# Attention and a routed expert layer on one core: where VectorE's routing operations stand, and who sends the results

## What is computed

```
Q = (x @ Wq.T).reshape(B, S, HKV, G, HEAD_DIM)          # K, V alike
scores = jnp.einsum('bskgd,bswkd->bskgw', Q, K_win) * scale
attn = jax.nn.softmax(scores, axis=-1)
out = jnp.einsum('bskgw,bswkd->bskgd', attn, V_win)
x = _layernorm(x + out.reshape(B, S, HQ * HEAD_DIM) @ Wo.T)
probs_BTE = jax.nn.softmax(x @ kernel_router_DE, axis=-1)
weights_BTX, indices_BTX = jax.lax.top_k(probs_BTE, TOP_K)
norm_weights_BTX = jax.nn.softmax(weights_BTX, axis=-1)
fuse_BTEF = jax.nn.silu(gating_BTEF) * jnp.einsum('BTD,EDF->BTEF', x, kernel_up_EDF)
down_BTED = jnp.einsum('BTEF,EFD->BTED', fuse_BTEF, kernel_down_EFD)
x = _layernorm(x + jnp.einsum('BTED,BTE->BTD', down_BTED, full_weights_BTE))
```

## Time and profile before

| | us |
|---|---|
| median of 3 runs (lowest, highest) | 593.84 (588.29, 595.39) |
| the profiled execution, its own time | 593.14 |
| its span in the trace | 591.3 |
| TensorE busy | 492.1 (83%) |
| VectorE busy | 359.9 (61%) |
| ScalarE busy | 297.9 (50%) |
| GpSimd busy | 241.4 (41%) |
| mean granted TensorE clock | 0.896 of full |

### The profile page before, as it was taken

One profiled execution on the slowest core, in us unless ns is written; L12 is line 12 of the kernel. 1 busy time (PEld: TensorE's weight loads), 2 busy tenths in 40 slices (PEclk: granted clock), 3 DMA queues, 4 the chain that ended last, 5 costly groups with the idle time before them and its releaser, 6 DMA issues.

```text
span 591.3 us, 12074 instructions
## 1 busy us (share of the span) xinstructions
PE 492.1 (83%) x3864; PEld 301.5 (51%) x3864; DVE 359.9 (61%) x817; ACT 297.9 (50%) x515; POOL 241.4 (41%) x329
## 2 busy tenths in 40 slices
PE   4499899899998999899898987966988999998600
PEld 3263454354453555344453533435877888886500
DVE  0366675576675887667756566553364635767674
ACT  2125554465566656456644544534565555554532
POOL 2131062462533225325435264305714517777072
PEclk9999898798999998899977877788889999999855
DMA  6452324305216352231350012020433535553252
GB/s 159 62 81 56 73 41 105 73 11 135 38 34 147 73 108 56 56 65 54 55 84 18 20 41 86 11 63 25 127 97 96 149 110 135 137 136 96 62 137 58
DMA packets 83948, 46.93 MB, mean 79 GB/s; under 512 B 40496, under 2 KB 79408, under 8 KB 83120
## 3 DMA queue, kind: packets, MB, share of 16 engines
q1 hardware_dynamic: 77184, 36.81, 27.2%
q0 software_dynamic: 4096, 8.40, 5.2%
q10 hardware_dynamic: 2608, 0.95, 0.8%
HBM read 26.47 MB, written 19.40 MB: 78 GB/s over the span
## 4 chain that ended last, share of the span: by engine, by line
PE 61%; DVE 15%; issue 8%; DMA 6%; ACT 3%; SPq 3%; POOL 2%; ACTq 0%; POOLq 0%; DVEq 0%
PE pV L788 13%; DVE mp L1311 6%; PE pX L977 6%; PE pX L713 5%; PE pX L957 4%; PE pX L752 4%; PE pX L959 4%; PE pX L958 3%; DMA xt<-xT 3%; PE pV L968 3%; DVE rden L1359 3%; PE pM L807 3%; PE pX L743 2%; PE pX L764 2%; SPq L427 2%
## 5 line engine op out<-in xcount | busy, mean ns | idle before, releaser
L1311 DVE TENSOR_REDUCE mp<-pX 128x4 f32<-128x1024 f32 (+4 forms) x128 | 150.2, 1186 | 96.6 <-PE pX L717 80.1
L1051 ACT ACTIVATE probs<-pX 128x1024 f32<-128x1024 f32 x152 | 152.8, 1023 | 108.7 <-PE pX L743 94.4
L788 PE MATMUL pV<-probs,vx 128*32 128x512 f32 (+1 forms) x736 | 94.4, 613 | 0.0
L660 POOL DMA_INDIRECT probs<-ys,source x64 | 64.1, 1002 | 48.1 <-issue 31.4
L648 POOL DMA_INDIRECT xs<-xr,slot x64 | 63.0, 984 | 49.5 <-DVE ends L1231 31.4
L752 PE MATMUL pX<-q,kx 50*128 50x512 f32 x248 | 64.5, 518 | 10.1 <-DVE mp L1311 9.4
L713 PE MATMUL pX<-kx,q 48*128 48x512 f32 (+4 forms) x256 | 62.1, 485 | 9.6 <-DMA q<-q_scr 9.6
L1402 DVE TENSOR_TENSOR probs<-probs,pX 128x512 f32<-128x512 f32 x44 | 30.2, 686 | 52.8 <-ACT probs L1108 52.7
L1108 ACT ACTIVATE probs<-pX 128x512 f32<-128x512 f32 x44 | 26.3, 598 | 53.6 <-PE pX L959 53.6
L713 PEld LDWEIGHTS pX<-kx,q 48*128 48x128 f32 x256 | 26.5, 205 | 50.9 <-issue 39.5
L977 PE MATMUL pX<-we,probs 128*128 x352 | 48.4, 282 | 0.7 <-ACT vx L1120 0.7
(11 more groups left out here) (151 smaller groups left out, 827.5 us busy)
## 6 DMA issues: line engine op xcount, KB each, us to landing
q<-q_scr SPq DMA_DIRECT2D x46, 128.0 KB, 4.4
xt<-xs SPq DMA_DIRECT2D x88, 64.0 KB
ys<-vx SPq DMA_DIRECT2D x44, 128.0 KB, 1.9
xt<-xT SPq DMA_DIRECT2D x8, 512.0 KB, 5.9
q_scr<-qh SPq DMA_DIRECT2D x32, 64.0 KB
q<-stage SPq DMA_DIRECT2D x128, 2.0 KB
xr<-x SPq DMA_DIRECT2D x8, 256.0 KB, 6.4
raw<-wgu SPq DMA_DIRECT2D x4, 512.0 KB, 5.5
```

What stands on the lines that cost most here:

```text
L660: pool.indirect_dma_start(yin[:, t % YIN, k, :], None, ys[ph][:, :], bass.IndirectOffsetOnAxis(ap=source[:, t, k:k + 1], axis=0), bounds_c ...
L788: mm = pe.matmul(pV[row:row + 32, cols], vx[:, chunk, pr, :], src[:, pr, cols], start=n == 0, stop=True, skip_group_check=True)
L1051: act.activation(dst, src[:], ACT.Exp).then_inc(exp_done, 1)
L1311: dve.tensor_reduce(mp[:, t % 2, 0, :, i, :], src[:, :, 0:2 * n].rearrange("p r (c v k) -> p r v c k", v=NV, k=32), AX.XY, ALU.max).then_i ...
```

## The change

Six things are edited.

1. In VectorE's step the second maximum (`largest_score(a, 1)`) now stands behind slot operations, table pieces, norm seeds and the first slot of routing, ahead of the third maximum; it stood ahead of all of them.
2. RT_AT is dealt out anew. Groups 0 and 1 take three steps instead of four (five operations ahead of the maxima in each of the second and third), so rank products, slots and sorting come one step earlier. Group 3, which is routed among the units, takes five steps instead of three, in slices of five or six.
3. Part 0's table goes into steps 27, 30 and 31 (5, 8 and 6 operations), the latter two behind attT; the tables of the other parts start at units 4 and 18 instead of 5 and 14.
4. TensorE makes the gate and up products of unit 0 inside step 32, ahead of the rank products and the output product of tile 31.
5. VectorE does step(MOE_STEPS[k]) behind the hidden of unit k instead of ahead of xl of unit k + 1 (unit 0 apart), and ScalarE does the routing exps behind the result of unit k - 2.
6. ScalarE sends each unit's result itself, behind the copy that makes it; SyncE sent it.

```diff
 for m_ in range(NT // RT_TILES):
     s_ = 8 * m_ + 15
     if m_ < NT // RT_TILES - 2:
-        RT_AT.update({s_: (m_, (0, 2), (2, 4), (4, 6)), s_ + 1: (m_, (6, 8), (8, 10), (10, 12)),
-                      s_ + 2: (m_, (12, 14), (14, 16), (16, 18)), s_ + 3: (m_, (18, 18), (18, 20), (20, 21))})
-        RANK_AT[s_ + 3] = m_
-        SLOT_AT[s_ + 4] = m_
+        RT_AT.update({s_: (m_, (0, 2), (2, 4), (4, 6)), s_ + 1: (m_, (6, 11), (11, 12), (12, 13)),
+                      s_ + 2: (m_, (13, 18), (18, 20), (20, 21))})
+        RANK_AT[s_ + 2] = m_
+        SLOT_AT[s_ + 3] = m_
...
-        BEHIND = XIN + 2
-        ZEROS_AT = (10, 20)
-        TABLE_AT = (5, 14)
+        TABLE_0 = {27: (0, 5), 30: (5, 13), 31: (13, TB_OPS)}
+        ZEROS_AT = (10, 22)
+        TABLE_AT = (4, 18)
...
-            def rows_made(k):
-                sp.wait_ge(y_done, k + 1)
-                ph, i = UNIT[k]
-                sp.dma_start(ys[ph].rearrange("(i h p) d -> i p h d", h=2, p=P)[i],
-                             ysb[:, k % YOUT]).then_inc(s_ys[k % YOUT], 16)
-
...
                 if has(s - 1):
                     sums(s - 1)
+                if s == NT:
+                    gate_up(0)
                 if projected(s) is not None:
...
                 act.copy(ysb[:, k % YOUT].rearrange("p h d -> p (h d)"), pX[2][:, 1, 0:2 * D]).then_inc(y_done, 1)
+                ph, i = UNIT[k]
+                act.wait_ge(y_done, k + 1)
+                act.dma_start(ys[ph].rearrange("(i h p) d -> i p h d", h=2, p=P)[i], ysb[:, k % YOUT]).then_inc(s_ys[k % YOUT], 16)
...
                     rows_made(k - 2)
+                if k and k in MOE_STEPS:
+                    routing_exps(MOE_STEPS[k])
...
-                largest_score(a, 1)
                 if s in SLOT_AT:
                     for n in range(SL_OPS):
                         slot_op(SLOT_AT[s], n)
-                for j in range(4):
-                    if s == 28 + j:
-                        for n in range(5 * j, min(5 * j + 5, TB_OPS)):
-                            table_op(0, n)
+                for n in range(*TABLE_0.get(s, (0, 0))):
+                    if s < 30:
+                        table_op(0, n)
...
                 for n in range(*ops[0]):
                     rt_op(m, n)
+                largest_score(a, 1)
                 largest_score(a, 2)
...
                     negated(a)
+                for n in range(*TABLE_0.get(s, (0, 0))):
+                    if s >= 30:
+                        table_op(0, n)
...
-                if k in MOE_STEPS:
+                if k == 0:
                     step(MOE_STEPS[k])
                 if k + 1 < NU:
                     rest_rows(k + 1)
                 hidden(k)
+                if k and k in MOE_STEPS:
+                    step(MOE_STEPS[k])
```

More of the change, by code:

```diff
@@ L551, in _ @@
                 rows_in(k)
-                if k >= BEHIND:
-                    rows_made(k - BEHIND)
-            for k in range(NU - BEHIND, NU):
-                rows_made(k)
             for b in range(NB):
@@ L667, in step @@
                 if s == 28:
-                    for t in range(8, 16):
+                    for t in range(12, 16):
                         sort_rows(t)
@@ L675, in step @@
                     sort_rows(s - 20)
+                if s == 27:
+                    for t in range(8, 12):
+                        sort_rows(t)
             for s in range(FIRST, NT):
```

33 lines of the change are left out of this document (19 added, 14 removed).

## The result

The changed kernel takes 576.5 us (median of 4 runs, 574.8 to 578.75) where the kernel before takes 593.75 (588.29 to 595.39): a ratio of 0.973, 95% interval 0.966 to 0.980. The forecast was 575 us. The profiled execution of the changed kernel is the longest of its four, 578.75 us, 14.4 less than the profiled one of before.

A forecast was written before the change was run, and what follows sets the result against it. TensorE was taken as the bound, losing time in attention to waits for VectorE's maxima and to half clock behind them. Gains of 1.8 + 11 + 1 + 4.4 = 18.2 us from 593.14 gave 575 us, range 566 to 587.

The forecast's parts named there:

- Attention, 1.8 + 11 us: Attention steps: 1.8 us gained from TensorE's waits for VectorE's maxima, 11 us from half-clock stretches behind them.
- charged 2.5 back: Attention: 1.5 us for slot, seed and routing operations too long for the gap, 1.0 us for earlier rank products.
- The rival that the clock does not follow the waits: Attention: half clock stays though the waits go; only 1.8 + 1 + 4.4 us gained, 586 us; chance 20%.
- The four fifths that I took: Attention: share taken of the 13.7 us gained if all five half-clock stretches behind waits go, giving 11 us.
- Into the units, +1: Passage from attention into the first units: unit 3's products start at about 412.5 instead of 413.49; gain 1 us.
- Leftover routing, +4.4: Units 8 to 13: routing in slices behind hidden k cuts the lost time from 7.1 to 2.7 us; gain 4.4 us.
- Left: 2.7 us: Units 8 to 13, loss remaining: 0.9 for table loads, 0.2, and 1.6 us for rank products at unit 12.
- the rival of late pieces: Postponed pieces are late on the path, costing 4 us more, and new gaps keep half clock; about 581 us; chance 10%.
- ScalarE issues ys, 0: Units: ScalarE sending each result, at about 0.5 us per issue and wait, costs 0 us.
- xl of unit k + 2, now about 1.7 us early: Units: what waits behind ScalarE's issue was taken to be about 1.7 us early, so cost 0.
- The rival of ScalarE as the bound: Units: issue and wait exceed the 1.1 us left, stretching all 44 units; 615 us at 2.0 us each; chance 5%.
- The last row, +1.5: Unit 41 to the end, last row of the gains by stretch; forecast 0, the tail taken as not touched.

The follow-up runs named there:

- e11: Kernel before with only the second maximum moved behind the slot, table, seed and first routing operations; 575.4 us, ratio 0.980.
- e3: Changed kernel with the second maximum back in front of the slot, seed and first routing operations; 597.4 us, ratio 1.013.
- e5: Changed kernel with unit 0's gate products behind step 32 again instead of inside it; 693.0 us, ratio 1.005, on a chip with standstills.
- e12: Changed kernel, results sent from SyncE again, last group's ranks and slots a unit later, seeds ahead of slot operations; 569.7 us, ratio 0.962.
- e6: Kernel before with only the second maximum moved behind slot, table, seed and first routing operations; 674.5 us, ratio 0.985, with standstills.
- e10: Kernel before with only the second maximum moved behind slot, table, seed and first routing operations, run again; 674.8 us, ratio 0.980, with standstills.
- e8: Changed kernel with eight useless copies between the first and second maximum of step 22; 689.5 us, ratio 1.006, with standstills.
- e1: Changed kernel with unit results sent from SyncE's queue again, eight units late; 574.9 us, ratio 0.966.
- e2: Kernel before with only the attention part of the change (order, routing of groups 0 and 1, part 0's table); 570.4 us, ratio 0.966.
- e9: Changed kernel, results from SyncE, last ranks and slots a unit later, seeds ahead of slot operations, run again; 679.0 us, ratio 0.992, with standstills.
- e7: Changed kernel, results from SyncE, last ranks and slots a unit later, seeds ahead of slot operations; 685.1 us, ratio 0.999, with standstills.
- e4: Changed kernel with the last routing group's rank products, slots and sorting one unit later; 570.8 us, ratio 0.967.

## Why the prediction was right where it was, and where not

- *Attention, 1.8 + 11 us.* The mechanism is right for the waits and right in part for the clock: the new order takes L752's wait away with either dealing (8.7 to 1.9 us in e11, 5.2 to 1.4 from e3 to the changed kernel). But in e11, where only the order is new and no such wait is over 1.0 us, steps 25 to 29 still run at clock 0.82 and the busy time falls by 3.0 us, of the 11.8 that order and dealing take together. The step that a half-clock stretch goes with the wait ahead of it does not hold by itself. Of the 18.3 us that the pair of profiles shows, 11.8 are busy time (177.5 to 165.6), against 11 taken from the clock, and 6.5 are idle time, against 1.8 taken from the waits. Before is one trace; against it the five with the attention of the change gain 14.7 to 18.3 us, of which 8.6 to 11.8 busy and 5.9 to 6.5 idle. The term mis-sized is the waits. I took 4.3 us as what could be gained, the excess of the late steps alone, and charged 2.5 back; L752's waits of steps 14 to 32 are 8.7 us, and 7.3 of them went. Of the charges, L752's product waits at most 0.3 us at a time now, and B4's wait grew from 4.0 to 5.3 us; the rank products waited 0.7 us, once. Whether the rest of the idle gain has a cause of its own (the waits for a projection's input, 1.5 us before, are absent after) was not tried.
- *The rival that the clock does not follow the waits* is refuted as a forecast of the sum, yet its core stands. e11 has nearly the idle time of the changed kernel (16.2 and 15.7 us) and 8.9 us more busy time; e3 falls to half clock behind slices in which TensorE was busy 6.43 of 6.8 us; and the same wait at unit 12 has half clock behind it in two traces of five. The four fifths that I took was a good number for a reason that the runs don't bear out. The Trainium skill ("TensorE: Matmul & The Clock Gate", "A second HAM failure mode: psum-queue depth-cycling") tells of a kernel whose clock swings between its two levels because TensorE idles shortly and often between groups of matmuls. e3's trace looks alike, with half clock in seven stretches of 6.8 us, whose starts lie 13.6 to 13.7 us apart, from 288 to 370 us. Which pattern of short waits starts it, these runs leave open.
- *The dealing of groups 0 and 1* had no gain of its own in the sum, only the rank products' 1.0 us as a charge. It should have had one: with the order it takes away 6 to 9 us of TensorE's busy time, and without it, it loses (7.7 us in e3's trace).
- *Into the units, +1.* Measured -0.2; over all traces without standstills 19.4 to 20.2 us with the change's units and seeds, 20.0 to 20.6 without, so 1 us is within what they leave open. As forecast, unit 2 starts 3.86 us behind unit 1 and TensorE stands idle ahead of tile 28, for 3.63 us. The gate products inside the step bring nothing (e5), because the gain is lost at tile 28; the seeds behind eight slot operations are half of that wait (e12).
- *Leftover routing, +4.4.* Measured -0.7 in the pair of profiles, and much of that is where half clock fell: before's units 8 to 13 have it too (clock 0.92), the changed kernel's more (0.86). At clock 1.00 the old order of the units takes 20.5 and 20.8 us (e6, e10, ahead of their next standstill) and the new one 20.5, 20.3 and 20.4 (e3, e5, e8). So the edit is worth nothing to 0.5 us, not 4.4. The step of the prediction that failed is "Left: 2.7 us": at clock 1.00 some 4.2 us are idle (20.4 less 16.2 busy), 1.3 of them the wait for msk, which was forecast at 1.6, and most of the rest pauses ahead of the gate products, up to 1.2 us, that the sum did not hold. The mechanism was right up to unit 11, where 2.1 us are gained (11.4 against 13.5 us from unit 8), and nearly all of it is lost again from unit 11 to 13 (9.0 to 9.1 against 7.1 to 7.3). The baseline was wrong too: of the 7 us that the prediction called lost some 1.7 were half clock. No term stood for half clock behind the wait at unit 12, only the rival of late pieces; it took 3 us in the changed kernel's trace, and the wait alone does not bring it, for e3, e5 and e8 have the wait without it.
- *ScalarE issues ys, 0.* Measured -3.9 in units 13 to 41, of which e1 gives back 3.4. The text had set 3.3 us a unit as the sign of being wrong, and it is 3.25, so the sign was set too wide: the loss of 3.9 us stays under it. The issue took 0.37 us, no more than forecast. The failed step is "xl of unit k + 2, now about 1.7 us early": that counts from the first product, but TensorE's queue needs the remainder 1.7 us ahead of it (its wait for the remainder, the turning and the table entries stand between), so nothing was free. The rival of ScalarE as the bound, with a room of 1.1 us, had the right place and the wrong form: no room was overrun, the handover became longer.
- *The last row, +1.5*, is within chance: the kernels with before's units and those with the change's both have 50.5 us there (e2, e3). *Units 3 to 8, -0.9*, repeats (17.7 to 18.0 us with the old units, 18.3 to 18.8 with the new) and is gone in e12 (18.0); its cause was not looked for.
- *The sum.* 575 us was hit with a gain in attention larger than forecast by up to 5.5 us, and units that lost 4.2 where 5.4 was to be gained. The waits of the largest term are borne out and its clock in part; the closeness of the total is luck.

## What to carry to other kernels

Put an engine's side work where that engine waits anyway, ahead of the operation that will be late for its own input, and not between that operation and the next one that another engine needs. A wait of TensorE on the path may have half clock behind it or not: take the wait alone and the wait with half clock as bounds, and before you price a stretch of some 20 us read it in several traces, since one profile can mistake 3 us of clock for an effect. Try order and dealing together and each alone: here the dealing paid only in the new order, and lost in the old. An engine with 44% of idle time can still be the wrong place for a DMA issue, if the wait for its own copy comes ahead of a handover.

## What the runs showed of the hardware

- Half clock can keep coming back at the same place of a loop, step after step, without a long wait (e3's slices). The same wait of 1.34 us had half clock behind it in two traces and none in three (unit 12).
- With the same order of operations up to there, the reciprocal of step 14 came at 185.7 us (e9) and 196.1 us (e10); from the first reciprocal on (52.1 and 53.1 us) the granted clock was 0.99 in e9 and 0.90 in e10. Where half clock falls moves a single execution by some 10 us.
- A product whose queue waits for VectorE's remainder, turns two blocks of rows and loads two table entries started at least 1.65 us behind the remainder, in every unit from 13 to 41 of the eight traces without standstills.
- On two chips all kernels took longer: before 91 to 97 us, the kernels with the three edits 109 to 115 us (e9, e7 against e12). TensorE stood still for 5 us or more five to seven times in each trace, 45 to 68 us in all, while GpSimd's indirect DMAs ran; the traces without the disturbance have no such pause behind the first 25 us. In e7's 18 us GpSimd went on issuing, and no packet of an instruction queue moved, where e4's 19 us had two. That the engines had run out of instructions fits this; it was not shown. The Trainium skill ("Runtime: NRT & Kernel Launch", "Instruction fetch mechanics") tells that an engine fetches its program in blocks by DMA and that this is mostly hidden. e4's two packets agree; whether e7's standstill is a fetch that was not hidden, no run here shows.
